# Post-norm attention with a routed feed-forward layer on one core: the diagonal mask of the row maxima moved from TensorE to VectorE, one queue for the last maxima, two tails in turn

## The reference, cut to what matters

```python
q, k, v = (x @ W.T + b for W, b in ...)                 # 16 heads, depth 8
scores = einsum('bqhd,bkhd->bhqk', q, k) * attn_scale[0]
scores = where(mask, -inf, scores)                      # keys after the query
out = einsum('bhqk,bkhd->bqhd', softmax(scores), v) @ Wo.T + bo
x = layernorm(x + out)
logits = x @ gate_weight.T                              # sigmoid, group top-4, top-6
for gu, dn, c in experts: acc += c * ((silu(x @ gu[:I].T) * (x @ gu[I:].T)) @ dn.T)
return layernorm(x + acc + shared(x))
```

## Time and profile before

| what | us |
|---|---|
| runs of the kernel (3) | median 483.38, 482.3 to 483.65 |
| the profiled execution | 482.52 |
| its span, first to last instruction | 480.8 |
| busy PE, DVE, ACT, POOL | 438.0, 352.1, 225.4, 141.6 |
| maxima reduced on DVE (line 987, 384 units) | 190.0 |
| mask on PE (line 1255, 128 matmuls) | 39.5 |

### The profile page before, as it was taken

The page is one execution under the profiler, slowest core; times in us unless marked ns, Lnnn a source line. Parts: engine busy times, 40 slices in busy tenths (PEclk is TensorE's granted clock), DMA queues, the critical chain, the costliest instruction groups (busy, mean ns, idle before and its releaser), DMA issues.

```text
span 480.8 us, 7765 instructions
## 1 busy us (share of the span) xinstructions
PE 438.0 (91%) x2665; PEld 210.1 (44%) x2665; DVE 352.1 (73%) x848; ACT 225.4 (47%) x302; POOL 141.6 (29%) x244
## 2 busy tenths in 40 slices
PE   5669999999999999999986988899999999999992
PEld 2422222323333332323232334567676676666660
DVE  2659978888988888797981464686768869855863
ACT  4520036576757767667635775523332342322220
POOL 4064412856656362514433425000000000000000
PEclk9955558999999999999999599899999999999997
DMA  3565126120101011000000004023333333442330
GB/s 120 181 207 159 33 69 205 29 86 3 49 29 42 29 35 35 3 1 1 3 2 3 0 9 87 28 106 100 104 81 102 106 89 103 133 142 89 115 104 22
DMA packets 27382, 34.22 MB, mean 71 GB/s; under 512 B 6096, under 2 KB 16464, under 8 KB 27344
## 3 DMA queue, kind: packets, MB, share of 16 engines
q1 hardware_dynamic: 26192, 33.00, 23.2%
q10 hardware_dynamic: 1152, 0.74, 0.6%
HBM read 29.07 MB, written 4.46 MB: 70 GB/s over the span
## 4 chain that ended last, share of the span: by engine, by line
PE 75%; DVE 12%; issue 5%; ACT 3%; POOL 2%; ACTq 2%; DMA 1%; DVEq 0%; SPq 0%; POOLq 0%
PE ps L1342 13%; PE ps L1259 13%; PE ps L1384 12%; DVE mx L987 9%; PE ps L1357 6%; PE ps L1359 6%; PE ps L1358 6%; PE ps L1255 6%; PE ps L1325 5%; PE ps L1221 2%; ACTq L571 2%; ACT probs L884 1%; PE ps L1272 1%; DVE x L1052 1%; DMA wq<-in_wqT 1%
## 5 line engine op out<-in xcount | busy, mean ns | idle before, releaser
L987 DVE TENSOR_REDUCE mx<-ps 128x2 f32<-128x256 f32 (+3 forms) x384 | 190.0, 552 | 37.5 <-PE ps L1259 36.0
L884 ACT ACTIVATE probs<-ps 128x1024 f32<-128x1024 f32 (+2 forms) x160 | 143.0, 940 | 73.0 <-PE ps L1325 66.4
L1259 PE MATMUL ps<-rows_k,rows_q 48*128 48x128 bf16 (+3 forms) x576 | 115.0, 304 | 5.1 <-DVE mx L987 3.0
L1342 PE MATMUL ps<-probs,Vg 128*32 128x512 f32 (+3 forms) x768 | 85.3, 518 | 1.5 <-POOL probs L758 1.4
L927 ACT ACTIVATE rows_q<-ps 128x512 f32<-128x512 f32 x68 | 40.5, 597 | 95.0 <-PE ps L1359 92.3
L1357 PE MATMUL ps<-x1hi,w_hi 128*128 128x512 f32 x136 | 74.6, 548 | 2.2 <-ACT work L913 2.2
L1259 PEld LDWEIGHTS ps<-rows_k,rows_q 48*128 48x128 bf16 x576 | 35.5, 97 | 90.9 <-DVE mx L987 67.4
L754 POOL TENSOR_SCALAR_AFFINE_SELECT probs<-probs 64x512 f32<-64x512 f32 x64 | 42.3, 662 | 111.2 <-ACT probs L884 109.8
L1325 PE MATMUL ps<-rows_q,rows_k 51*128 51x512 bf16 (+3 forms) x384 | 69.1, 343 | 3.0 <-ACT probs L884 2.9
L1384 PE MATMUL ps<-rows_k,w_down 128*128 128x512 f32 x136 | 69.7, 595 | 0.7 <-DVE rows_k L1203 0.7
L1198 DVE TENSOR_TENSOR rows_q<-ps,rows_q 128x512 f32<-128x512 f32 x64 | 44.1, 689 | 34.9 <-PE ps L1384 34.6
(11 more groups left out here) (105 smaller groups left out, 328.0 us busy)
## 6 DMA issues: line engine op xcount, KB each, us to landing
comb_rows<-weights SPq DMA_DIRECT2D x128, 128.0 KB, 2.9
scratch<-oT SPq DMA_DIRECT2D x8, 384.0 KB, 2.6
w_raw<-in_unitT SPq DMA_DIRECT2D x17, 128.0 KB, 2.4
rows_q<-scratch SPq DMA_DIRECT2D x16, 96.0 KB
rows_k<-scratch SPq DMA_DIRECT2D x14, 96.0 KB
w_down<-in_unitT SPq DMA_DIRECT2D x1, 1088.0 KB, 6.7
xT<-in_xT SPq DMA_DIRECT2D x4, 256.0 KB, 5.7
rows_q<-scratch SPq DMA_DIRECT2D x16, 64.0 KB
```

Source lines behind the costliest of these rows:

```text
L884: act.activation(dst, src, ACT.Exp).then_inc(exps_ready, 1)
L987: dve.tensor_reduce(to, src, AX.X, ALU.max).then_inc(max_read, 1)
L1259: mm = pe.matmul(dst[:, at * m:(at + 1) * m], rows_q[f:f + ROWS, s, p + qt * P:p + (qt + 1) * P], rows_k[f:f + ROWS, s, p + k0:p + k0 + m] ...
L1342: mm = pe.matmul(ps[STRIP * j:STRIP * (j + 1), VALUES * BANK:VALUES * BANK + m], Vg[:, g % 2, kt, j, :], probs[:, (NB * g + b) % SLOTS, j, ...
```

## The change

Units of maxima are cut anew: a part 0 of up to 512 keys from the diagonal on and a part 1 of the rest. For the first six query tiles a unit of part 0 holds one head, PE writes bare scores, and DVE adds a mask tile (`score_mask`, zero behind its first 128 columns) and takes the maximum in one instruction, whose full result goes to one of four scratch tiles. Tiles 6 and 7 keep two heads a unit and the mask on PE, now 128 columns for each head and after its scores. The maxima have two parts instead of three. For the last group SP issues all twelve DMAs of each half. The tails of chunk 0 and chunk 1 are laid in turn, chunk 1 by 4.5 steps behind, with a second buffer for `att`, `attT` and `ex`. The planner's costs follow.

```diff
-        for part, most in ((0, P), (1, BANK), (2, BANK)):
+        for part, most in ((0, BANK), (1, BANK)):
             m = min(n, most)
             if m:
-                units += [(js, qt, k0, m, part) for js in ([(0, 1), (2, 3)] if 2 * m <= BANK else [(0,), (2,), (1,), (3,)])]
+                paired = 2 * m <= BANK and (part or qt >= PE_MASKS)
+                units += [(js, qt, k0, m, part) for js in ([(0, 1), (2, 3)] if paired else [(0,), (2,), (1,), (3,)])]
+PE_MASKS = 6
...
-    return steps + tail + [(kind, 1, i) for kind, i in CHUNK_STEPS[:ROUTED]]
+    tails = [(k, 0, step) for k, step in enumerate(CHUNK_STEPS)]
+    tails += [(k + CHUNK_LAG, 1, step) for k, step in enumerate(CHUNK_STEPS[:ROUTED])]
+    return steps + [(kind, n, i) for _, n, (kind, i) in sorted(tails)]
+CHUNK_LAG = 4.5
...
-                if TOPS[g][1] is not None:
-                    todo["act"].append(("rows", g, 0, end + hop, 2000))
...
-                t += len(js) * max(m / 2.4 + 10, 105) + 120 * (part == 0)
-                dve = max(dve, t + hop) + len(js) * m / 0.96 + 125
+                t += len(js) * (max(m / 2.4 + 10, 105) + 105 * (part == 0 and len(js) > 1))
+                dve = max(dve, t + hop) + len(js) * m / 0.96 + (155 if part == 0 else 125)
...
                 else:
-                    store_half(sp, t, 0)
+                    for f in range(2):
+                        store_half(sp, t, f)
...
+            pool.memset(score_mask[:, :], 0.0).then_inc(mask_set, 1)
+            pool.wait_ge(mask_set, 1)
+            pool.wait_ge(masks_loaded, 32)
+            pool.tensor_copy(score_mask[:, 0:P], mask_qk[:, :]).then_inc(mask_set, 1)
...
-            def store_tops(t):
-                act.wait_ge(max_split, t + 1)
-                store_half(act, t, 1)
...
-                dve.tensor_reduce(to, src, AX.X, ALU.max).then_inc(max_read, 1)
+                if part == 0 and per == 1:
+                    k = fused.index(NM * g + n)
+                    if k >= 4:
+                        dve.wait_ge(max_read, fused[k - 4] + 1)
+                    dve.tensor_tensor_reduce(masked_scores[k % 4][:, 0:m], src[:, 0, :], score_mask[:, 0:m], 1.0, LAST, ALU.add,
+                                             ALU.max, to).then_inc(max_read, 1)
+                else:
+                    dve.tensor_reduce(to, src, AX.X, ALU.max).then_inc(max_read, 1)
...
-                if part == 0:
-
-                    pe.matmul(dst.rearrange("p (j m) -> p j m", m=m), identb[:, :],
-                              mask_qk[:, :].unsqueeze(1).to_broadcast([P, len(js), P]), start=True, stop=False)
                 for at, j in enumerate(js):
                     f, p = ROW_HALF * (j // PAIRS), j % PAIRS * T
+                    by_pe = part == 0 and len(js) > 1
                     mm = pe.matmul(dst[:, at * m:(at + 1) * m], rows_q[f:f + ROWS, s, p + qt * P:p + (qt + 1) * P],
-                                   rows_k[f:f + ROWS, s, p + k0:p + k0 + m], start=part > 0,
-                                   stop=part > 0 or at == len(js) - 1)
+                                   rows_k[f:f + ROWS, s, p + k0:p + k0 + m], start=True, stop=not by_pe)
+                    if by_pe:
+                        mm = pe.matmul(dst[:, at * m:at * m + P], identb[:, :], mask_qk[:, :], start=False, stop=True)
```

## The result

The changed kernel takes 464.1 us (median of four, 462.6 to 466.1) against 483.5 us before (four, 482.3 to 483.9): a ratio of 0.9605, 95% interval 0.9564 to 0.9647. The forecast said 464.5. The profiled execution took 462.63 us, its span 460.9; before it was 482.52 and 480.8. Medians here are over all executions of a kernel, while ratios and their intervals leave out those more than 1.5% above the fastest one of their kernel, and of the experiments a2 and b3 no rows are used, because their profiled execution was one of those.

The account below looks back on a forecast made before the run. Maxima bound by PE and DVE handing three PSUM banks to and fro, the tail by latencies, the loop by PE. 482.5 - 9.5 - 4 - 5 = 464.0, with half of 0.9 us 464.5 us; own range 457 to 469, wider range 452 to 478.

Parts of the forecast that it names:

- part 1: Row maxima, masks of six tiles moved from PE to DVE: 9.5 us saved in all.
- price d of a fused unit: Extra DVE time of a fused mask-and-maximum unit over a plain one: 0.075 us, range 0 to 0.14.
- idle time left over: DVE's idle time in a group of maxima after the change: 2.0 us, bounds 0.6 and 2.6.
- fused units' sharing of SBUF with POOL: DVE's fused units using SBUF beside POOL's mask selects: costed at nothing.
- worse bound: Rival in the maxima: fused unit costs over d = 0.22, kernel gets slower, 497 us at d = 0.30; chance 0.07.
- DVE becomes the bound: Groups of maxima: PE's chain part falls to about 20 us, so DVE, at 24.5 us a group, bounds.
- Part 2: Last maxima's stores: SyncE alone issues them, freeing ACT but making POOL's second split wait; 4 us saved, bounds 0 and 9.
- part 3: Tails of both chunks laid in turn before the expert loop: 5 us saved, bounds 1 and 7.
- POOL's second split stalls the tail: Rival: serial stores cancel ACT's gain, or first routing holds the loop; both tail changes give 2 us, total 471; chance 0.13.
- start to start 0.70: Sign in the profile after: successive fused units on DVE begin 0.70 us apart.
- A group near 26.5: Sign in the profile after: a head group of maxima has a period near 26.5 us.
- The loop 45 to 47 us after the last maximum: Sign in the profile after: the expert loop starts some 45 to 47 us after the last maximum.

Follow-up runs that it names:

- a2: Changed kernel with ACT again issuing half of the last maxima's stores: 465.26 us, ratio 0.9646.
- b3: Changed kernel with its 40 units a group, TensorE adding all masks again and DVE taking plain maxima: some 493 us, ratio 1.0211.
- a4: Changed kernel with units, mask and planner's unit costs of before put back; SyncE's stores and the tails in turn stay: 470.03 us, ratio 0.9741.
- b2: Changed kernel with plain maxima in place of the fused units, first six tiles' mask left out: 459.73 us, ratio 0.9523.
- b4: Changed kernel with a two-column DVE copy, which nobody reads, behind each fused unit: 492.53 us.
- c2: Changed kernel with a separate place for the last maxima's second half, and tiles 6 and 7 masked on DVE too: 459.25 us, ratio 0.9495.
- c4: Changed kernel with a separate place for the last maxima's second half, but ACT again issuing half of the last stores: 464.15 us, ratio 0.9618.
- b1: Changed kernel with the last maxima's second half split into a place of its own (second buffer), so POOL need not wait: 455.0 us, ratio 0.9438.
- a1: Kernel before with only the new units and DVE masks; ACT still stores half, tails one after the other: 471.92 us, ratio 0.9798.
- a3: Changed kernel with the second tail behind the first again: 465.62 us, ratio 0.9651.
- c0: Changed kernel measured once more without an edit, on another occasion: 460.44 us, ratio 0.9492.
- c3: Changed kernel with a separate place for the last maxima's second half, but the tails one after the other: 462.45 us, ratio 0.9572.

## Why the prediction was right

The time was right to 0.4 us, and that is in part luck: part 1 brought more than its term and the tail less, and the two errors cancelled. The mechanisms of the three parts came as written; TensorE's clock, which moved the time by some us in either direction, was no term of the sum.

**Part 1's size.** Forecast: six groups 8.4 us, the second 1.5, the first a loss of 0.4. Six groups brought 10.55 us in both profiled executions of the changed kernel (27.86 to 26.10 each). The second took 26.65 us at a clock of 0.67 and 28.17 at 0.60; with the units of before it took 28.31 at 0.67 (a4) and 29.81 at 0.62, so 1.6 to 1.7 us at a like clock. The first, from its first maximum to its join, gained 1.0. Two terms of the group were off. The price d of a fused unit was taken as 0.075 us and is 0.009 (b2): DVE's busy time is 23.22 us a group and not 24.5. (Of these 1.3 us d accounts for 1.6; the other units need 0.3 more than the sum's 22.66.) The idle time left over is 26.10 - 23.22 = 2.9 us and not 2.0, near the "2.6 at the present rates" that the prediction worked out and then shortened. The two nearly cancel: -1.3 and +0.9. With d = 0 the prediction expected about 18 us of part 1; d is nearly 0, and part 1 alone brought 10.5. The fused units' sharing of SBUF with POOL, costed at nothing, was right: their mean is 686 ns.

Here the Trainium skill helps to read the row. "VectorE: DVE Perf Modes", section "Two Vector instructions with no wait between them", says that an accumulator output is two instructions; the trace agrees (83 ns for the second). The Trainium skill's "Vector Engine (DVE) Microarchitecture Reference", section "5.2 Measured stream behaviour on trn2", puts a fixed cost of about 75 ns on an instruction. Adding that for the read, as the prediction did with the like value from its rows, was wrong here: by the rows the read and the next unit start together.

**The slope of the sum.** The prediction let d pass straight into the group, 22.66 + 24d + 2, and into the first group, 24d - 1.39. b4 tests this with copies that cost 0.16 us each. The first group from its first maximum to its join, in before, after and b4:

```profile
28.45:53.76 25.31, 24.08 (x91) 6.84 (x90) 23.70 (x50) 0.00 (x0) 14.01 (x20) 0.50 0.51 160
28.87:53.14 24.27, 22.96 (x59) 5.42 (x58) 22.79 (x66) 0.00 (x0) 14.17 (x20) 0.50 0.52 166
29.18:57.34 28.16, 23.48 (x59) 5.43 (x58) 26.71 (x90) 0.00 (x0) 14.32 (x20) 0.50 0.47 144
```

From after to b4 DVE's busy time grew by 3.92 us and the group by 3.89, all three at the same clock: here the slope is as the sum has it. Of the six groups, the two of b4 at a clock of 0.93 to 0.94 grew by 3.6 and 3.9 us over the same groups of the changed kernel, DVE's busy time by 4.0. The other four ran at 0.79 to 0.85 and grew by 5.6 to 7.3 us; no term of the sum has that. b4 is slower than before with some 0.17 us a fused unit, so the rival "worse bound" set its point, d > 0.22, too high, and what it lacked is mostly the clock.

A group is a hand-over between two engines that are both nearly full. Time added to PE counts in full (b3); time taken from PE counts only as far as DVE lets it, and c2, without gain at full clock, says that this point is reached. "DVE becomes the bound" was right in that sense. The shares of the chain do not say it: over the six groups the chain reads mostly PE in both kernels, first before, then after.

```profile
by line: PE ps L1342 29.5%; PE ps L1259 25.1%; DVE mx L987 14.9%; PE ps L1325 10.9%; PE ps L1255 10.5%; issue 4.2%; ACTq L571 1.8%; PE ps L1245 0.8%; ACT probs L884 0.7%; POOL mh L773 0.3%; POOL mh L769 0.3%; POOL mh L777 0.3%; POOL mr L775
```

```profile
by line: PE ps L1357 29.1%; PE ps L1273 24.5%; DVE comb_rows L1001 15.0%; PE ps L1340 9.9%; issue 8.5%; PE ps L1276 4.5%; DVE mx L1004 2.8%; SPq L581 1.9%; DVE mx L1001 1.7%; PE ps L1262 0.5%; POOL mh L788 0.3%; POOL mh L784 0.3%; POOL mh L
```

What the chain's mask matmuls lost is as much as the six groups gained: before (L1255) 10.5% of 167.16 us, after (L1276) 4.5% of 156.61, 17.55 - 7.05 = 10.5 us. That is a match of two sizes and no test: c2 took these last mask matmuls away and gained nothing.

**Part 2's size.** The mechanism came as written: no DMA on ACT, SP's twelve stores 0.61 us apart, POOL's second split behind them (it waits 5.05 us and begins 5.45 us after the last maximum; forecast 5.3 and 6.1), selects and PE's values behind that. ACT's freedom is worth 8.6 us with its clock (c4 against b1), of the 10.9 that the prediction counted; it charged 4 for POOL and halved the rest. Measured, POOL's wait costs some 2.8 us by itself and 4 to 10 us with the clock that falls behind it. The kernel before paid for its clock too: it ran at 0.50 from 265.68 to 273.18, after PE had stood 3.41 us ahead of 263.25, behind ACT's second wait. The net came out at 7 us from a1 to a3 and at 2 and 7 us from a2 to the changed kernel and c0, by the ratios. The forecast's 4 us lie between them, but the clock was no term of the sum. The rival "POOL's second split stalls the tail" was thus half right: its mechanism is there; its 471 us would have needed part 3 to fail as well.

**Part 3** was right: 5.0 to 6.2 us from the last exponential to the loop in every pair (12.58 or 11.76 to 6.42, 11.69 to 6.68, 11.67 to 6.42), its one table load ahead of the first down matmul, the first routing's store hidden (the first wait for its rows is 0.5 us), and the loop unchanged: 172.2 us against 172.8.

**The signs named ahead.** Fused units of 0.69 us with a short second instruction: yes; start to start 0.70: no, 0.61. A group near 26.5: 26.10. DVE idle near 2: 2.9. POOL late: yes. The loop 45 to 47 us after the last maximum: no. By the loop step at which the prediction cut it, 51 us (54.4 before); the hole and the clock are in it, since with the second buffer the first down matmul comes 41.8 us after the last maximum, against 52.4 in the kernel after.

**What stays open.** Why the hole brings the clock down in four profiled executions and not in a4; why single groups fall below 1.00 in every profiled kernel with part 1 and in none without it (before, a4); which of POOL's instructions hold up a DVE copy, since beside some of them a copy stays short. The second buffer's 455.0 us is the best median of the study. It ran on another chip than c0; by the ratios it is 0.5% (2.6 us) under c0, with intervals that overlap, and 1.7% (8 us) under the changed kernel on record.

## What to carry to other kernels

An engine that waits a few microseconds on another's in-order queue can cost more than the wait when TensorE is behind it: price the half clock afterwards as a term of its own, with a chance, and look for a second buffer before accepting a wait that "only" moves. Before trusting a sum for two engines that hand banks to and fro, ask for the slope of each, since the chain's shares name who came last and not what a microsecond more on either would cost; a dummy step measures it, once the trace has said what the dummy itself costs. And a forecast whose total is right can rest on terms that are wrong together: cut the trace at fixed rows and compare the terms.

## What was not expected of the hardware

- The accumulator's read, 83 ns, starts together with the next unit: 0.61 us from start to start of fused 128x512 units, as for plain maxima. A copy of two columns in the same place moves the next unit to 0.68, and 36 of 192 such copies last up to 0.93 us, each until 0.02 to 0.03 us after the end of a POOL instruction. The fused units, PSUM and SBUF in, did not slow down beside POOL (mean 686 ns).
- The granted clock is at 0.50 for about 5 us after PE had stood for most of 3 to 4 us (245.80 to 251.37, rows above), in the kernel after, and stays at 1.00 behind a like hole in a4. In the three profiled executions without the hole (b1, c3, c2) the tail is at 1.00.
- Groups run below full clock in the kernels that took mask work from PE: one group of the six at 0.94 in the kernel after, 0.82 in a group of c2, 0.79 in one of b4, against 1.00 in all six of before. That the lighter or more interrupted work of PE is the cause is not shown: in c2 the next group, with the same units, ran at 1.00 and was 3 us shorter.
